# Mixture of experts in one block: sort inverted by one-hot products, rows gathered and scattered tile by tile

## The chip, the cores and the metric

One core of a Trainium2 chip runs the whole kernel. It has TensorE (PE; its weight loads are shown as PEld), VectorE (DVE), ScalarE (ACT), GpSimd (POOL) and SyncE (SP), each with an instruction queue of its own, and 16 DMA engines that all of them can start transfers on. The metric is the device time of one execution in microseconds (us), lower is better.

## The reference

The kernel runs eight stages over 4096 tokens (16 sequences of 256) of 128 channels. Two of the eight, the second and the fourth, are the same mixture of experts; they share their weights. Names and sizes are those of the inputs.

```
feats  = layernorm(x)                                  # (4096, 128)
scores = feats @ centroids.T                           # (4096, 8)
expert = argmax(scores, axis=1)
alpha  = sigmoid(sum(feats * centroids[expert]))
h      = layernorm(feats) * gamma[expert] + beta[expert]
y      = feats + relu(h @ W1[expert].T + b1[expert]) @ W2[expert].T + b2[expert]
x      = x + alpha * y + (1 - alpha) * feats
```

W1 and W2 are 512x128 and 128x512 for each of the 8 experts, all float32. With feats taken out of y, the last line is x + feats + alpha * (relu(...) @ W2.T + b2), which is how the kernel forms it.

## The kernel before

The tokens lie in SBUF as `env.X`, 32 blocks of 128 tokens (NT = 32), and in chunks of four blocks (NC_ = 8). Each stage ends with `sweep` (line 31), a barrier of all engines. Within the expert stage (tags e1 and e3, `experts`, line 865) there are blocks that end with a barrier each:

- `row_scales` (135): DVE and ACT work out mean, scale and shift of each token from its statistics. SP issues five small parameter loads, and behind them the 16 loads of W1 and W2; the block waits for the small ones.
- `turn_weights` (97): two transposes of small parameters.
- `choose` (914): DVE normalises rows chunk by chunk, TensorE transposes them (line 271), ACT copies them out of PSUM, TensorE forms the scores (938), and DVE finds the best expert (967 to 979).
- `place` (982): TensorE counts the tokens per expert and block (1011) and then transposes all weights (1018), ACT copies those out of PSUM (1031). DVE works out each token's slot in an order sorted by expert, every expert's run padded to whole tiles of 128 (1061 to 1079), 40 tiles in all (NJ = 40). It waits before that for memsets of POOL (1035 to 1040). Then it normalises the rows again (1081), and POOL scatters them to the DRAM buffer `sorted_rows` with 32 indirect transfers (1047). In the first stage the buffer is cleared before (1103). SP reads the sorted rows back as `ZS` (1109). Meanwhile beta is folded into b1 by 32 products (1023) and gamma into W1 by DVE (1092, 1093).
- `sorted_experts` (1113): the 40 tiles, in a loop of two tiles per round. TensorE in order: `turn(j + 1)` transposes the next tile's rows (1135), `first(j)` makes the 512 hidden values (1145), `second(j - 1)` the output (1157) and adds b2 by one more product with a row of ones (1159). ACT copies the tile's rows (1189), evacuates the transpose (1202), does half of the relu (1181) and copies b2 and W2 of the tile's expert (1195, 1196). DVE copies b1 and W1 of the expert (1229, 1230), does the other half of the relu (1179) and copies the finished tile to `YS` (1234). SP stores `YS` in four parts to `sorted_out` (1261).
- `collect` (1265): POOL gathers the tokens' rows out of `sorted_out` with 32 indirect transfers (1278), four per chunk; DVE waits for each chunk and adds it, scaled, to X (303, 314), and forms the next statistics (320).

Waits are by semaphores: `need` puts the wait on the following instruction, `hold` on an instruction of its own. `Link` makes each DVE step wait for the one before it. Each engine runs its queue in order, so an instruction that waits holds up all behind it.

## Time and profile before

| | us |
|---|---|
| median of 3 runs | 3189.96 (3188.9 to 3190.61) |
| the profiled execution | 3196.09 |
| its span in the trace | 3194.4 |
| first expert stage (e1) | 661.0 to 926.0 |
| second expert stage (e3) | 1330.2 to 1588.8 |
| TensorE busy | 2303.7 (72%) |
| DVE busy | 2372.1 (74%) |
| ACT busy | 1595.5 (50%) |
| POOL busy | 1677.2 (53%) |

How to read the rows: a row of the timeline has start, busy time, engine, line, operation, what it writes `<-` what it reads, partitions x elements, and how many instructions were merged (float products on TensorE count twice, since they take two passes). In brackets stands the idle time of the engine before it and what ended it. Times are us from the span's start. "Issue" in a bracket is time in which the engine waited for nothing that the profile shows. In the stretches, each engine's busy time and number of instructions is given, then the granted TensorE clock as a share of 2.4 GHz (0.50 is 1.2 GHz).

### The profile page before, as it was taken

How to read it: one execution, taken by the hardware profiler on the slowest of the kernel's cores; microseconds unless marked ns; L12 is line 12 of the kernel's file. 1: busy time of each engine (PE TensorE's matmuls, PEld its weight loads, DVE VectorE, ACT ScalarE, POOL GpSimd, SP SyncE). 2: the span in 40 equal slices, each digit the busy share in tenths (PEclk: the TensorE clock that was granted, in tenths of full speed). 3: DMA queues.
4: the chain of work that ended last, by engine and by line, in shares of the span. 5: the costliest groups of instructions: out<-in, count | busy, mean ns of one | idle time of the engine just before them, and what ended most of it. 6: DMA issues, size and time to landing. Idle time of an engine off the chain costs nothing. (4 is left out here: it accounts for less than half of the span.)

```text
span 3194.4 us, 60389 instructions
## 1 busy us (share of the span) xinstructions
PE 2303.7 (72%) x16660; PEld 1733.3 (54%) x16660; DVE 2372.1 (74%) x5812; ACT 1595.5 (50%) x3215; POOL 1677.2 (53%) x1416
## 2 busy tenths in 40 slices
PE   6727777764929999749244887588888656888887
PEld 2302222343818888638243665476777534777676
DVE  4469999843556666535458886599999876999998
ACT  2356666522715555327223555366666533666665
POOL 0079999703030000040325555499999503999996
PEclk9959999966959999859677999699999956999999
DMA  1000000022110000120100000100000000000000
GB/s 47 0 0 1 0 0 0 1 86 59 32 54 1 0 0 0 54 59 22 51 1 1 1 0 1 30 1 0 0 0 0 3 0 1 1 0 0 0 0 27
DMA packets 61386, 42.73 MB, mean 13 GB/s; under 512 B 7795, under 2 KB 55940, under 8 KB 61190
## 3 DMA queue, kind: packets, MB, share of 16 engines
q1 hardware_dynamic: 56070, 32.09, 3.5%
q0 software_dynamic: 4096, 8.40, 0.9%
q10 hardware_dynamic: 1120, 1.06, 0.1%
q8 instruction: 44, 0.72, 0.1%
q14 instruction: 56, 0.46, 0.0%
HBM read 27.38 MB, written 14.16 MB: 13 GB/s over the span
## 5 line engine op out<-in xcount | busy, mean ns | idle before, releaser
L1631 POOL TENSOR_TENSOR k7a_psums<-k7a_sims 128x1024 f32<-128x1024 f32 x224 | 423.2, 1915 | 189.4 <-ACT k7a_sims L1737 159.2
L1631 POOL TENSOR_TENSOR k5a_psums<-k5a_sims 128x1024 f32<-128x1024 f32 x224 | 423.1, 1915 | 78.2 <-ACT k5a_sims L1737 47.5
L1691 PE MATMUL k7a_pw<-g_ident,k7a_w 128*128 128x128 f32 x2048 | 272.6, 279 | 87.9 <-DVE k7a_hid L1823 47.9
L1691 PE MATMUL k5a_pw<-g_ident,k5a_w 128*128 128x128 f32 x2048 | 273.1, 279 | 86.8 <-DVE k5a_hid L1823 47.9
L755 POOL TENSOR_TENSOR mc_hc<-mc_h,mc_cs 128x512 f32<-128x512 f32 x256 | 319.9, 1270 | 12.7 <-PE mc_y L645 5.1
L728 DVE TENSOR_TENSOR_SCAN mc_h<-mc_dA,mc_dbu 128x512 f32<-128x512 f32 x256 | 304.6, 1208 | 0.0
L1691 PEld LDWEIGHTS k5a_pw<-g_ident,k5a_w 128*128 128x128 f32 x2048 | 224.1, 142 | 147.2 <-DVE k5a_w L1814 91.5
L1691 PEld LDWEIGHTS k7a_pw<-g_ident,k7a_w 128*128 128x128 f32 x2048 | 223.4, 141 | 148.1 <-DVE k7a_w L1814 92.3
L1814 DVE SCALAR_TENSOR_TENSOR k5a_w<-k5a_psums,k5a_best,k5a_lift 128x1024 f32<-128x1024 f32 x224 | 279.4, 1271 | 0.6 <-ACT k5a_lift L1752 0.2
L1814 DVE SCALAR_TENSOR_TENSOR k7a_w<-k7a_psums,k7a_best,k7a_lift 128x1024 f32<-128x1024 f32 x224 | 279.2, 1271 | 0.2
L1752 ACT ACTIVATE k7a_lift<-k7a_psums 128x1024 f32<-128x1024 f32 x224 | 227.8, 1027 | 87.2 <-DVE k7a_w L1814 85.9
L1752 ACT ACTIVATE k5a_lift<-k5a_psums 128x1024 f32<-128x1024 f32 x224 | 227.8, 1027 | 86.0 <-DVE k5a_w L1814 84.7
L645 PE MATMUL mc_y<-mc_hc,g_ident 128*128 128x512 f32 x512 | 242.9, 597 | 11.8 <-DVE m_sz L710 11.6
L1035 POOL MEMSET e3l_keep<- 128x256 f32 x1 | 0.3, 313 | 450.9 <-POOLq L918 450.9
L675 ACT ACTIVATE mc_dA<-m_delta,m_A 128x510 f32 (+1 forms) x256 | 176.7, 690 | 118.6 <-DVE mc_h L728 118.3
L1278 POOL DMA_INDIRECT e_YS<-sorted_out,e_slot x64 | 60.6, 947 | 258.8 <-PEq L1268 239.9
L2155 ACT ACTIVATE r4a_pr<-r4a_pst 128x384 f32<-128x384 f32 x256 | 111.6, 488 | 121.0 <-PE r4a_pst L2311 119.7
L2221 POOL TENSOR_SCALAR_AFFINE_SELECT r4a_pr<-r4a_pr 128x256 f32<-128x256 f32 x256 | 103.0, 420 | 120.4 <-ACT r4a_pr L2155 120.3
L632 PE MATMUL mc_B<-m_bc,g_sel 96*128 (+1 forms) x128 | 50.4, 393 | 157.3 <-ACT mc_cs L687 87.8
L632 PEld LDWEIGHTS mc_B<-m_bc,g_sel 96*128 96x128 bf16 x128 | 12.4, 97 | 253.3 <-issue 122.5
L645 PEld LDWEIGHTS mc_y<-mc_hc,g_ident 128*128 128x128 f32 x512 | 96.6, 190 | 97.5 <-issue 59.1
L2428 DVE TENSOR_REDUCE r4a_nm<-r4a_work 128x2 f32<-128x512 f32 (+1 forms) x192 | 121.4, 682 | 19.7 <-PE r4a_work L2282 19.5
(591 smaller groups left out, 6160.3 us busy)
## 6 DMA issues: line engine op xcount, KB each, us to landing
e_ZS<-sorted_rows SPq DMA_DIRECT2D x8, 640.0 KB, 7.1
sorted_out<-e_YS SPq DMA_DIRECT2D x8, 640.0 KB, 3.6
e1p_w<-in_L_ffn_W_dram SPq DMA_DIRECT2D x16, 256.0 KB, 5.2
e3p_w<-in_L_ffn_W_dram SPq DMA_DIRECT2D x16, 256.0 KB, 5.4
sorted_rows<-e_ZS SPq DMA_DIRECT2D x1, 2560.0 KB, 10.8
g_X<-in_L_attn_a_x_dram SPq DMA_DIRECT2D x8, 256.0 KB, 6.3
out_dram<-g_X SPq DMA_DIRECT2D x1, 2048.0 KB, 8.7
sorted_rows<-e_YS,e_slot POOLq DMA_INDIRECT x64, 2.2
```

The source lines that it names most:

```text
L632: nc.tensor.matmul(Bp[:, s % 2, :], env.sel[:, s, :], bc[:, cols], start=True, stop=True)
L645: nc.tensor.matmul(yp[:, h, :], env.ident[:, :], hc[:, q % RH, :], start=(s == 0), stop=False,).then_inc(summed, 1)
L675: nc.scalar.activation(dA[:, q % RD, :, 1:SEQ], d[:, :, 1:SEQ], ACT.Exp, scale=A[:, h, s:s + 1]).then_inc(decay, 1)
L728: nc.vector.tensor_tensor_scan(h_[:, q % RB, :], dA[:, q % RD, :, :].rearrange("p s t -> p (s t)"), dbu[:, q % RI, :], 0.0, ALU.mult, ALU. ...
L755: nc.gpsimd.tensor_tensor(hc[:, q % RH, :], h_[:, q % RB, :], cs[:, s % 2, :], ALU.mult).then_inc(outs, 1)
L1631: nc.gpsimd.tensor_tensor(psums[:, h - 1, :, :], rows_of(p, h), s2, ALU.add).then_inc(pooled, 1)
L1691: ins = nc.tensor.matmul(pw[:, j, :], w[:, h % WR, j * P:(j + 1) * P], env.ident[:, :], start=(h == 0 and j % 4 == 0), stop=(h == HD - 1 a ...
L1752: nc.scalar.activation(lift[:, h % LR, :], sums_of(h), ACT.Relu).then_inc(lifted, 1)
L1814: nc.vector.scalar_tensor_tensor(w[:, h % WR, :], sums_of(h), best[:, p, h, 7:8], lift[:, h % LR, :], ALU.is_ge, ALU.mult).then_inc(weighe ...
L2155: nc.scalar.activation(pr[:, h, :, :].rearrange("p b c -> p (b c)"), pst[:, h % 2, 0:3 * P], ACT.Exp).then_inc(expd, 1)
L2221: nc.gpsimd.affine_select(pr[:, h, 0:3:2, :], pr[:, h, 0:3:2, :], [[0, 2], [1, P]], ALU.is_ge, 0.0, base=0, channel_multiplier=-1).then_in ...
L2428: nc.vector.tensor_reduce(dst, src, AX, ALU.max, negate=True).then_inc(maxed, 1)
```

## The change

- **One block.** `choose`, `place`, `sorted_experts` and `collect` become one block per stage, with no barrier inside; loops over chunks and blocks are written out. POOL's short memsets come at once, the clearing of the DRAM buffer is gone.
- **Weights kept.** `expert_weights` loads and transposes the weights in the first stage only, and keeps them in SBUF until the last expert stage. Of the 16 groups of four transposes, four are issued ahead of the counts (EARLY), the rest behind them. b2 is loaded to all partitions.
- **The sort is inverted on TensorE.** Instead of scattering rows to slots, the kernel works out which token stands in each slot: a slot is split into tile and place; `hotq` says for each block which tile a token goes to, times its token number plus one (POOL multiplies), `hotr` which place. 32 products of 128x128 by 128x40, summed in PSUM, give `ids`, and from it `token`: row 0 for reading (empty slots read row 0), row 1 for writing (empty slots go to rows that nobody reads).
- **Gather and scatter beside the products.** The normalised rows `zn` go to DRAM by token. Per tile, POOL gathers its rows by token number to one of four buffers `zs` (RZ = 4), and scatters the finished tile to `token_out`. POOL's order is gather 0 to 3, then scatter(j), gather(j + 4) for each j.
- **In the tile loop**, now four tiles per round, gamma and beta are applied by the ACT step that evacuates the transpose (per-partition scale and bias in `affine`, which DVE copies for each tile), ACT no longer copies the rows, and b2 is added by DVE when it evacuates the output, not by TensorE. ACT's `hold` before it copies b2 and W2 is on `kept`, no longer on `summed`.
- **Return.** DVE applies keep and shift to all of X in place; when the last scatter has landed, SP loads the outputs, in token order, in eight transfers, and DVE adds them.

```diff
+    if env.expert_weights is not None:
+        row_scales(nc, env, tag + "sc", second)
+        return env.expert_weights, None
...
-            for t in range(NT):
-                pool.wait_ge(formed, t + 1)
-                nc.gpsimd.indirect_dma_start(env.sorted_rows[:, :], bass.IndirectOffsetOnAxis(slot[:, t:t + 1], 0),
-                                             rows[:, t, :], None).then_inc(scattered, 16)
...
+            pool.wait_ge(vec, SPLIT)
+            nc.gpsimd.tensor_tensor(hotq[:, :, :], hotq[:, :, :], over(env.steps[:, 2, 0:NT], NJ),
+                                    ALU.mult).then_inc(spread, 1)
+
+            def gather(j):
+                need(pool, zturned, j + 1 - RZ)
+                nc.gpsimd.indirect_dma_start(zs[:, j % RZ, :], None, env.token_rows[:, :],
+                                             bass.IndirectOffsetOnAxis(token[:, 0, j:j + 1], 0)
+                                             ).then_inc(gathered[j % RZ], 16)
+
+            def scatter(j):
+                pool.wait_ge(kept, j + 1)
+                nc.gpsimd.indirect_dma_start(env.token_out[:, :], bass.IndirectOffsetOnAxis(token[:, 1, j:j + 1], 0),
+                                             ys[:, j % RZ, :], None).then_inc(stored[j % RZ], 16)
+
+            pool.wait_ge(rowed, 16 * NC_)
+            pool.wait_ge(vec, TOKEN)
+            for j in range(RZ):
+                gather(j)
+            for j in range(NJ):
+                scatter(j)
+                if j + RZ < NJ:
+                    gather(j + RZ)
...
+            pe.wait_ge(spread, 1)
             for t in range(NT):
+                pe.wait_ge(compared, t + 1)
+                nc.tensor.matmul(ids[:, 0:NJ], hotr[:, t % (NT // 2), :], hotq[:, t, :], start=(t == 0),
+                                 stop=(t == NT - 1)).then_inc(found, 1)
...
-                nc.tensor.matmul(po[:, p, 0:P], ones[:, :], b2s[:, p, :], start=False, stop=True).then_inc(summed, 1)
...
+                nc.scalar.activation(zT[:, p, :], pz[:, p, 0:P], ACT.Identity, bias=affine[:, p, 1:2],
+                                     scale=affine[:, p, 0:1]).then_inc(z_in, 1)
...
+            def keep_rows(it, z):
+                j = it * RZ + z
+
+                need(dve, stored[z], 16 * it)
+                need(dve, summed, j + 1)
+                nc.vector.tensor_tensor(ys[:, z, :], po[:, z % 2, 0:P], b2s[:, z % 2, :], ALU.add).then_inc(kept, 1)
...
+            for z in range(RZ):
+                sp.wait_ge(stored[z], 16 * (NJ // RZ))
+            for n in range(NC_):
+                ts = slice(n * TPC, (n + 1) * TPC)
+                sp.dma_start(own[:, ts, :], outs[:, ts, :]).then_inc(loaded[n], 16)
```

On POOL, what stands in a row in the first expert stage before, from the last memsets to the end of the stage (`e_slot` are the slots, `e_YS` the rows):

```order
-L1037 MEMSET e_ones 1x128
-L1038 MEMSET e_ZS 128x5120
-L1040 MEMSET e1l_keep 128x8
-L1047 DMA sorted_rows<-e_YS,e_slot 5120x128 x32
-L989 UNCONDITIONAL_BRANCH
-L1275 UNCONDITIONAL_BRANCH
-L1278 DMA e_YS<-sorted_out,e_slot 128x128 x32
```

and now, up to the third tile:

```order
+L1111 MEMSET e_keep 128x8
+L1114 TENSOR_TENSOR e_hotq<-e_hotq,g_steps 128x1280
+L1119 DMA e_zs<-token_rows,e_token 128x128 x4
+L1125 DMA token_out<-e_ys,e_token 9216x128
+L1119 DMA e_zs<-token_rows,e_token 128x128
+L1125 DMA token_out<-e_ys,e_token 9216x128
+L1119 DMA e_zs<-token_rows,e_token 128x128
```

The large memset has gone, all scatters used to stand before the tiles and all gathers behind them, and now they alternate through the tiles.

On TensorE, from the counts of the first expert stage to the first tile, before:

```order
-L1011 MATMUL e1l_counts<-e1p_hot,g_ranks 128x256 x2
-L1018 MATMUL e1l_turned<-g_ident,e1p_w 128x128 x64
-L1023 MATMUL e1l_shifts<-e_byexpert,e_w1T 128x8 x32
-L989 UNCONDITIONAL_BRANCH
-L1129 UNCONDITIONAL_BRANCH
-L1135 MATMUL e1e_pz<-g_ident,e1e_zs 128x128 x2
-L1145 MATMUL e1e_ph<-e1e_zT,e1e_w1s 128x128 x4
```

and now, up to the output of the first tile (`e_hotr`, `e_hotq` are the one-hots, `e_po` their sum):

```order
+L973 MATMUL e_ph<-g_ident,e_w 128x128 x16
+L991 MATMUL e_ph<-e_hot,g_ranks 128x256 x2
+L973 MATMUL e_ph<-g_ident,e_w 128x128 x48
+L999 MATMUL e_po<-e_hotq,e_hotr 128x40 x32
+L1010 MATMUL e_pz<-g_ident,e_zs 128x128 x2
+L1021 MATMUL e_ph<-e_zT,e_w1s 128x128 x4
+L1010 MATMUL e_pz<-g_ident,e_zs 128x128
+L1021 MATMUL e_ph<-e_zT,e_w1s 128x128 x4
+L1034 MATMUL e_po<-e_w2s,e_hid 128x128 x4
```

16 of the weight transposes have moved ahead of the counts, the 32 products with 8 columns are replaced by 32 with 40, and within a tile the order turn, first, second is as before, without the product for b2.

## Rows read from the trace of the kernel before

**Rows 1.** The head of the page: span and number of instructions.

```profile
span 3194.4 us, 60389 instructions
```

**Rows 2.** Stretches of e1: bounds, length, busy us (instructions) of PE, PEld, DVE, ACT, POOL, clock, DMA.

```profile
698.40:773.00 74.60, 23.95 (x132) 21.55 (x131) 24.16 (x70) 12.54 (x67) 36.66 (x37) 0.57 0.34 99
773.00:875.50 102.50, 101.43 (x760) 91.31 (x760) 54.56 (x200) 75.63 (x239) 0.00 (x0) 0.97 0.06 20
875.50:926.00 50.50, 0.00 (x0) 0.00 (x0) 25.07 (x96) 0.00 (x0) 30.30 (x32) 0.52 0.20 55
```

**Rows 3.** The same stretches of e3, and the end of its scale steps (timeline).

```profile
1330.20:1344.50 14.30, 0.39 (x2) 0.28 (x2) 3.31 (x18) 1.92 (x4) 0.00 (x0) 0.56 0.80 247
1367.30:1437.00 69.70, 23.86 (x131) 21.44 (x131) 24.61 (x70) 12.58 (x67) 36.46 (x37) 0.57 0.24 68
1538.40:1588.80 50.40, 0.00 (x0) 0.00 (x0) 25.11 (x96) 0.00 (x0) 30.32 (x32) 0.52 0.20 55
...
1334.21 0.19 DVE L187 SCALAR_TENSOR_TENSOR g_rnorm<-e3sc_tmp,g_rstd 128x32 f32<-128x32 f32 x1
```

**Rows 4.** Timeline of e1, one steady tile: start, busy, engine, line, operation.

```profile
819.29 0.33 PE L1135 MATMUL e1e_pz<-g_ident,e1e_zs 128*128 128x128 f32 x1
819.46 1.06 PE L1145 MATMUL e1e_ph<-e1e_zT,e1e_w1s 128*128 128x128 f32 x8
820.35 1.06 PE L1157 MATMUL e1e_po<-e1e_w2s,e1e_hid 128*128 128x128 f32 x8
821.34 0.48 PE L1159 MATMUL e1e_po<-e1e_b2s,e_ones 1*128 1x128 f32 x2
821.75 0.33 PE L1135 MATMUL e1e_pz<-g_ident,e1e_zs 128*128 128x128 f32 x1
...
822.02 0.29 DVE L1234 COPY e_YS<-e1e_po 128x128 f32 x1
```

**Rows 5.** Timeline of e1, DVE from the choice of the expert to the slots.

```profile
700.73 0.42 DVE L977 TENSOR_TENSOR e1p_hot<-e1r_sc,e1r_m 128x256 bf16<-128x256 f32 x1
...
707.14 0.42 DVE L1061 COPY e1l_per<-e1l_counts 128x256 f32<-128x256 f32 x1 [5.76 <-POOL e1l_keep L1040]
...
712.21 0.18 DVE L1079 CAST e_slot<-e1l_slotf 128x32 int32<-128x32 f32 x1
```

**Rows 6.** Groups by form, POOL: count | busy us, mean ns | idle before.

```profile
L575 POOL TENSOR_TENSOR m_du<-m_delta,m_u 128x1024 f32<-128x1024 f32 x4 | 10.3, 2579 | 9.5 <-DVE m_delta L594 9.5
```

**Rows 7.** Timeline of TensorE, products with few columns in two stages.

```profile
2016.73 7.01 PE L1305 MATMUL k5w_out<-k5p_keysT,k5p_wq 128*128 128x32 f32 x32 [0.77 <-PEq L101]
...
714.93 11.45 PE L1023 MATMUL e1l_shifts<-e_byexpert,e_w1T 128*128 128x8 f32 x64 [0.35 <-ACT e_w2T L1031]
```

**Rows 8.** Timeline of e1, return: fourth gather of a chunk, and DVE's steps.

```profile
884.05 0.95 POOL L1278 DMA_INDIRECT e_YS<-sorted_out,e_slot  x1 [0.30 <-issue]
...
886.59 1.12 DVE L303 TENSOR_SCALAR e1c_kept<-g_X,g_keep,g_shift 128x128 f32<-128x128 f32 x4 [11.09 <-DMA e_YS<-sorted_out,e_slot]
887.74 1.18 DVE L314 SCALAR_TENSOR_TENSOR g_X<-e_YS,e_alpha,e1c_kept 128x128 f32<-128x128 f32 x4
...
888.95 0.87 DVE L320 BATCH_NORM_STATS2 g_stats<-g_X 128x6 f32<-128x128 f32 x4
```

**Rows 9.** DMA issues: count, size of each, median us from issue to landing.

```profile
e1p_w<-in_L_ffn_W_dram SPq DMA_DIRECT2D x16, 256.0 KB, 5.2
```

**Rows 10.** Timeline of e3: first normalised rows, and the first scatter.

```profile
1381.57 0.35 DVE L1081 TENSOR_SCALAR e_YS<-g_X,g_mean,g_rnorm  x1 [0.37 <-DVE e_slot L1079]
...
1382.72 1.01 POOL L1047 DMA_INDIRECT sorted_rows<-e_YS,e_slot  x1 [6.86 <-DVE e_YS L1081]
```

**Rows 11.** Timeline of e1: a scatter beside DVE steps in SBUF, and one without.

```profile
728.95 0.96 POOL L1047 DMA_INDIRECT sorted_rows<-e_YS,e_slot  x1 [0.31 <-DVE e_YS L1081]
...
730.12 0.47 DVE L1093 TENSOR_SCALAR e_w1T<-e_w1T,e_byexpert 128x512 f32<-128x512 f32 x1
730.21 1.21 POOL L1047 DMA_INDIRECT sorted_rows<-e_YS,e_slot  x1 [0.30 <-issue]
```

**Rows 12.** Stretches in other stages: PE's busy time and the granted clock.

```profile
948.00:960.00 12.00, 9.45 (x34) 6.32 (x34) 7.15 (x26) 5.90 (x10) 0.00 (x0) 0.50 0.00 0
2045.00:2048.00 3.00, 0.87 (x8) 0.80 (x8) 2.31 (x4) 2.95 (x4) 3.00 (x3) 1.00 0.00 0
```

More of the change, by code:

```diff
@@ new lines, in experts, with after, before, over @@
+        loaded = [sem(f"loaded{n}") for n in range(NC_)]
+        back = Back(nc, env, sb, ps, sem)
+        block = outer.enter_context(nc.Block())
+        HOT, ARG, COUNTS, SPLIT, TOKEN = 6, 7, 16, 23, 30
+        EARLY = 4
+        own = zn
+        def after(it, z):
+            return (it, z + 1) if z + 1 < RZ else (it + 1, 0)
+        def before(it, z):
+            return (it, z - 1) if z else (it - 1, RZ - 1)
+        def over(x, n):
+            return x.rearrange("p (k o) -> p k o", o=1).broadcast_to([P, x.shape[1], n])
@@ L982, in place @@
-def place(nc, env, tag, hot, slot, expert, ZS, rows, ones, NJ, weights):
-    NT = env.NT
-    E, J, BANKS = 8, 4, 4
-    fetched, landed, turns, w1T, b1, gT, bT = weights
-    with ExitStack() as ctx:
-        sb, ps, sem = scope(nc, ctx, tag + "l")
-        per, incl, at = sb("per", [P, E, NT]), sb("incl", [P, E, NT]), sb("at", [P, E, NT])
-        keep = sb("keep", [P, E, NT])
-        above = sb("above", [P, E, NT])
-        tiles, ends, one8, first = sb("tiles", [P, E]), sb("ends", [P, E]), sb("one8", [P, E]), sb("first", [P, E])
-        below = sb("below", [P, NJ, E - 1])
-        slotf, expertf = sb("slotf", [P, NT]), sb("expertf", [P, NJ])
-        counts, turned, shifts = ps("counts", [P, 2, 512]), ps("turned", [P, BANKS, 512]), ps("shifts", [P, E, J, E])
-        counted, set_, vec, formed, scattered, loaded, cleared, placed, evacuated, shifted, folded = (sem(x) for x in (
-            "counted", "set", "vec", "formed", "scattered", "loaded", "cleared", "placed", "evacuated", "shifted",
-            "folded"))
-        block = ctx.enter_context(nc.Block())
-        CLEAR = not env.sorted_rows_written
-        env.sorted_rows_written = True
-        GROUPS = 4
-        @block.tensor
-        def _(pe):
@@ L1256, in _ @@
[L1256 to L1287 removed]
+            rows = env.token_rows.rearrange("(t p) c -> p t c", p=P)
@@ L1290, in products @@
+            for n in range(NC_):
+                sp.wait_ge(loaded[n], 16)
 def products(nc, env, tag, items):
```

495 lines of the change are left out of this document (236 added, 259 removed).

## The prediction

> **What bounds the kernel now.** The kernel is a chain of stages with a barrier of all engines between them, so an expert stage is worth exactly what its own chain takes of the 3194.4 us [rows 1]. I read the busy time by stretches first, to cut the two expert stages (e1 from 661.0 to 926.0, e3 from 1330.2 to 1588.8) into routing, tiles and return. In e1 the scores end at 698.4, and the first tile's transpose starts at 773.0: 74.6 us, in which no engine but POOL is busy for half the time [rows 2]; in e3 the same is 69.7 us, and 14.3 us pass before its first normalised rows [rows 3]. The 40 tiles take 102.5 and 101.4 us with TensorE busy throughout. The return takes 50.5 and 50.4 us (875.5 to 926.0; in e3 from 1538.4 to the stage's end at 1588.8), and POOL issues 32 gathers in it [rows 2].
>
> Then I read the order of time inside the three. A steady tile takes TensorE 2.46 us: transpose (0.17 from its start to the next), first product 0.89, second 0.99, bias product and what follows 0.41 [rows 4]. So the tile loop is TensorE's; everything else in the stage is waiting for a chain over DVE, POOL and DMA.
>
> **Routing (front).** The change deletes the scatter of 32 row blocks, the reading back of the sorted rows, the shifts and scaling of W1, and the clearing. What is left in e1 from the end of the scores: choosing the expert ends 2.75 us after 698.4; the counts then stand behind 16 weight transposes that TensorE takes first, so that DVE's next step starts at about +4.5 (before it was 707.14, held by a memset on POOL) [rows 5]. From there to the slots it is 712.39 - 707.14 = 5.25 [rows 5]. New: four small linked steps at about 0.22 (a cast is 0.18 [rows 5], and its wait), and a comparison of 1280 elements, which at DVE's pace in [rows 5] (256 in 0.42, some 1 element per ns) is 1.5: 2.4 together. POOL's product of 1280 elements: 1024 take 2.58 [rows 6], so 3.1 (from 2.4 to 3.6). Then 32 float products with 40 columns, two passes each. The nearest rows are 32 passes of 32 columns in 7.01, 0.219 each, and 64 passes of 8 columns in 11.45 straight behind the weight transposes, 0.179 each [rows 7]. I take 11.4 for e1, which comes out of its transposes in the same way, and 14.0 for e3, which has none before. The 32 comparisons on DVE (at most 0.28 each by the 128x128 steps of [rows 8]) hide behind them. Token numbers: four small steps and a wait, 1.2. First gather: 0.80 until POOL starts it, 2.54 until it has landed (both below). Sum for e1: 4.5 + 5.25 + 2.4 + 3.1 + 11.4 + 1.2 + 3.3 = 31.2 against 74.6: **-43.4**. For e3 33.5 (2.6 more for the products, no transposes ahead of the counts) against 69.7: -36.2. Because the weights are kept, e3 also loses the wait for parameter loads and SP's 16 weight issues: the scale steps alone end at 1334.4 [rows 3], 4.2 after 1330.2, and with about 0.9 for the barrier that is 5.1 instead of 14.3: -9.2. In e1 the loads stay (b2 is moved behind the small ones), nothing is gained. Front of both: **-88.8**. The scores themselves stay TensorE's with the same passes; unrolled and in one block they may gain or lose 1.
>
> **Return (tail).** Before, POOL issued 32 gathers, one per 1.25 us, and DVE waited for each group of four. Now the rows are already in token order, and SP loads them with eight plain transfers. After the last kept tile DVE has 32 steps on X: four in 1.12 [rows 8], so 8.9, then eight chunks of 1.18 + 0.87 + gaps = 2.1 [rows 8], 16.8, and 1.2 to the next stage. Sum 26.9 against 50.5 and 50.4: **-47.1**. What covers the transfers: the last scatter starts 0.8 later and lands within 2.5, a 256 KB transfer lands in 5.2 [rows 9], so the first chunk is there after 8.5, just before DVE is through with X; if that cover fails it costs 1 to 3 per stage.
>
> **Tiles.** Here the change takes off and adds. Off: the bias product (0.41 on TensorE; its addition moves into DVE's evacuation, which takes the place of a copy of 0.29 [rows 4]) and ScalarE's copy of the rows. Scale and bias ride on the ScalarE step that was a copy. If TensorE alone decided, a tile would take 2.05. Added: 40 gathers and 40 scatters on POOL, strictly in the order scatter(j), gather(j+4). Their issue alone is 0.95 + 0.30 and 1.01 + 0.30 [rows 8, 10], or 2.56 per tile, already above 2.46. But there is a longer wait. scatter(j) waits for kept(j); gather(j+4) is queued behind it on POOL, although its data and buffer are long ready. TensorE's turn(j+4) waits for that gather, and behind turn(j+4) on TensorE are queued first(j+3) and second(j+2). DVE waits for second(j+2) to keep tile j+2, and that releases scatter(j+2). So one round of this chain spans **two** tiles:
> - TensorE from turn to the end of second: 0.17 + 0.89 + 1.06 = 2.12 [rows 4];
> - to DVE's start 0.20 (821.82 to 822.02), and its evacuation 0.29 [rows 4];
> - DVE's end to POOL's start of a scatter: 0.80 (1381.92 to 1382.72) [rows 10];
> - the scatter's issue, until the gather can start: 1.31, and 1.51 while DVE copies in SBUF, as it does there with the next W1 (POOL 1.21 instead of 0.96 busy beside such steps) [rows 10, 11]; I take 1.40;
> - the gather from its start to the engine that waits for it: 884.05 to 886.59, 2.54 [rows 8].
>
> Sum 7.35, or 3.68 per tile, and 147 us for 40 tiles (the first four are prefetched, but the pipeline fills at the low clock; I set one against the other). Against 102.5 and 101.4: **+90.1**. Bounds: if of the 0.80 only the usual 0.30 of a queued issue remains and the scatter is 1.31, 6.8, or 3.4 per tile; if both DMAs are slowed by DVE and register waits on TensorE add 0.3, 8.0, or 4.0 per tile. That is -22 and +26 on the total.
>
> What the skill adds here: the Trainium skill, "SBUF — State Buffer", section "SBUF: two separate sides", says that DVE's fast copies and POOL share one pair of ports as an exclusive lock for the whole instruction, and that descriptors written by POOL starve meanwhile. The trace agrees in kind (1.21 for 0.96); by the rule a whole such step (0.47 [rows 11]) could be added per round instead of 0.09, which would make the total 15 us longer. The Trainium skill, "DMA: Bandwidth & Descriptors", section "Anatomy of one DMA — SWDGE (gpsimd) path", gives about 2.0 us plus bytes over 436 GB/s per transfer, an estimate of 2.15 us for 64 KB; the row shows 2.54, and by the page the total would be 16 us shorter.
>
> **The sum.** The profiled execution is 3196.09 us (span 3194.4); the median is 3189.96, 6 lower, and I subtract from the median. -88.8 - 47.1 + 90.1 = -45.8, so 3190 - 46 = **3144**. The larger constant table loaded at launch and the longer unrolled code get at most 1 to 3.
>
> **Rivals.**
> - POOL's issue is the bound, not the round: the latencies overlap in some way I don't see. Then a tile takes 2.56, the loops take 102 each as before, and the total is 3190 - 136 = 3054. For it: four row buffers look like enough. Against: the queue order on POOL, which puts each gather behind a scatter that waits. Chance 6%; another 5% for something between 2.6 and 3.4 (3115 to 3060).
> - Slower: TensorE's clock. Its granted clock is 0.97 in the tiles of before [rows 2], where TensorE never pauses. Now it pauses 1.5 us in every 3.7. If it falls to 1.2 GHz, 2.12 becomes 4.24, the round 9.5, a tile 4.74 and a loop 190: 85 us more, **3229**. Everything above breaks even at 4.25 per tile. For it: a stretch of 12 us with TensorE 79% busy stayed at 0.50 [rows 12]. Against: a stretch of 3 us with only 0.87 busy kept 1.00 [rows 12], so pauses of this length don't take the clock away once it is there, and the first tiles come from prefetched rows with no pause, in which it should rise. Chance 13%.
> - The routing is not as short as I make it: POOL's product and DVE's comparisons disturb each other, the 40-column products run like full ones. At most 8 us per stage, 3160; inside my range.
>
> **Chances.** The forecast's own case (3.4 to 4.0 per tile, front and tail within 8) 71%, giving 3112 to 3179. Between 4.0 and 4.25 per tile 5%. The range has to take in part of the slow case's side: 3105 to 3200. About 0.2% is what a measurement of this kernel tells from no change. Faster by more 0.83, within 0.03, slower 0.14.
>
> **What would show it.** In the profile after: the first gather of e1 some 28 us after the scores; the same tile lines spaced 3.7 us with TensorE idle until the DMA of the gathered rows; POOL idle until DVE's kept tile, twice per round; 26 to 28 us from the last kept tile to the next stage. Wrong if the tiles are 2.5 apart with POOL never idle (first rival), or if TensorE's granted clock in them reads below 0.7 (second).

## The result, and the profile after

The changed kernel takes 3150.7 us (median of four runs, 3144.65 to 3151.4) beside 3189.57 us before: ratio 0.987, 95% interval 0.9856 to 0.9883. That is 38.9 us less; 45.8 were forecast (3144 us), and the range of 3105 to 3200 holds it. The profiled execution has a span of 3149.2 us, 45.2 less than the one before [rows 1]; the one before lay 6.5 us above its median (3196.09), so the profile shows more gain than the medians do.

The stretches of the profile answer to [rows 2, 3] (bounds, length, busy us and instructions of PE, PEld, DVE, ACT and POOL, granted clock, share of the DMA engines, GB/s): first front, tiles and return of the first expert stage, then of the second.

```profile
662.00:730.50 68.50, 45.26 (x228) 42.02 (x228) 33.02 (x118) 17.26 (x30) 5.34 (x6) 0.57 0.35 101
730.50:883.00 152.50, 104.51 (x680) 94.13 (x680) 61.61 (x235) 73.23 (x200) 76.85 (x77) 0.88 0.13 33
883.00:909.00 26.00, 0.00 (x0) 0.00 (x0) 24.27 (x97) 0.00 (x0) 0.97 (x1) 0.56 0.30 86
1314.30:1371.90 57.60, 34.58 (x163) 33.54 (x163) 32.76 (x117) 7.86 (x13) 5.17 (x6) 0.52 0.14 38
1371.90:1521.40 149.50, 101.64 (x680) 90.61 (x680) 62.20 (x235) 72.64 (x200) 76.94 (x77) 0.91 0.13 34
1521.40:1547.30 25.90, 0.00 (x0) 0.00 (x0) 24.15 (x96) 0.03 (x1) 1.03 (x1) 0.56 0.31 86
```

Set against the bounds of before (front 661.0 to 773.0 and 1330.2 to 1437.0, tiles 102.5 and 101.4, return 50.5 and 50.4):

| part | forecast | measured, both stages |
|---|---|---|
| front | -88.8 | -43.5 and -49.2: -92.7 |
| tiles | +90.1 | +50.0 and +48.1: +98.1 |
| return | -47.1 | -24.5 and -24.5: -49.0 |
| sum | -45.8 | -43.6 |

The other 1.6 us of the 45.2 lie outside the two stages. The tiles take back some two thirds of what the front and the return give, so most of the study looks at them.

What the tile loop waits for stands in the answers on two of its lines: the transposes of gathered rows (TensorE's matmul records alone, and what ended its waits ahead of them: us, times), and the scatters (count | busy us, mean ns | POOL's idle time ahead of them, and what ended it):

```profile
L1010 PE MATMUL e_pz<-g_ident,e_zs x80: 272/328/477, 730.6 to 1514.5; 128*128 128x128 f32 x80
its engine sat idle before it (us, times) until:
  DMA e_zs<-token_rows,e_token: 101.2, 62
```

```profile
L1125 POOL DMA_INDIRECT token_out<-e_ys,e_token x80 | 79.2, 990 | 126.1 <-DVE e_ys L1227 123.0 <-issue 3.0
```

TensorE waits for the gathered rows (101.2 of the 302 us of the two loops), POOL waits for the evacuated ones (123.0): neither is busy throughout, which is the mark of a ring, and not of an engine that is full. One turn of it at the full clock (timeline of the first stage: start, busy, engine, line, operation; tile j's evacuation, its scatter, the gather queued behind it, the transpose that this gather releases):

```profile
748.67 0.33 PE L1010 MATMUL e_pz<-g_ident,e_zs 128*128 128x128 f32 x1 [1.45 <-DMA e_zs<-token_rows,e_token]
749.97 1.06 PE L1034 MATMUL e_po<-e_w2s,e_hid 128*128 128x128 f32 x8
751.13 0.29 DVE L1227 TENSOR_TENSOR e_ys<-e_po,e_b2s 128x128 f32<-128x128 f32 x1 [0.35 <-PE e_po L1034]
751.70 0.99 POOL L1125 DMA_INDIRECT token_out<-e_ys,e_token  x1 [1.43 <-DVE e_ys L1227]
753.00 0.97 POOL L1119 DMA_INDIRECT e_zs<-token_rows,e_token  x1 [0.30 <-issue]
755.96 0.33 PE L1010 MATMUL e_pz<-g_ident,e_zs 128*128 128x128 f32 x1 [1.80 <-DMA e_zs<-token_rows,e_token]
```

748.67 to 755.96 is 7.29 us for two tiles. Over whole loops the scatters are 3.74 and 3.66 us apart on average.

### The profile page after: what moved, and what is told of

The parts are those of the page before. It is cut to its first block and busy times, and to the rows that moved or that the text cites. A ratio compares the mean times of both kernels' runs of the same rounds, so it can differ in the third digit from the quotient of the medians.

```text
span 3149.2 us, 59016 instructions
## 1 busy us (share of the span) xinstructions
PE 2296.4 (73%) x16434; PEld 1728.9 (55%) x16434; DVE 2378.4 (76%) x5875; ACT 1574.1 (50%) x3022; POOL 1709.6 (54%) x1446
## 3 DMA queue, kind: packets, MB, share of 16 engines
q10 hardware_dynamic: 1120, 1.22, 0.2%
## 5 line engine op out<-in xcount | busy, mean ns | idle before, releaser
L1125 POOL DMA_INDIRECT token_out<-e_ys,e_token x80 | 79.2, 990 | 126.1 <-DVE e_ys L1227 123.0
```

The source lines that it names most:

```text
L1125: nc.gpsimd.indirect_dma_start(env.token_out[:, :], bass.IndirectOffsetOnAxis(token[:, 1, j:j + 1], 0), ys[:, j % RZ, :], None).then_inc(s ...
```

## Experiments

The kernels ran in three groups of four, each group on one chip, and the three chips are different ones, here called A, B and C. The kernel before took 3204.8, 3193.8 and 3192.7 us on them. That turned out to matter, so totals are compared inside a group where that is possible, and it is said where not. Each version was traced once on its chip. Two of them leave something out of the result, to find a cause: the plain copy leaves out b2, the fixed expert the choice of the expert for VectorE's copies. "Loop" below is from the first transpose of gathered rows to the end of the last evacuation.

| kernel | chip | loops, us | clock in them | median, us | ratio to before (95%) |
|---|---|---|---|---|---|
| gather first | A | 128.6, 128.4 | 0.93, 0.94 | 3104.07 | 0.969 (0.9674 to 0.9706) |
| eight buffers | A | 127.8, 127.3 | 0.93, 0.94 | 3099.76 | 0.9674 (0.9657 to 0.969) |
| filled pauses | A | 144.2, 145.3 | 0.98, 0.97 | 3136.1 | 0.9789 (0.9773 to 0.9805) |
| weights loaded again | A | 150.3, 149.2 | 0.91, 0.91 | 3156.41 | 0.9854 (0.9836 to 0.9872) |
| X steps early | B | 153.4, 148.7 | 0.88, 0.92 | 3144.07 | 0.9839 (0.9823 to 0.9855) |
| eight buffers, copies early | B | 100.0, 99.6 | 0.97, 0.97 | 3041.17 | 0.9522 (0.9506 to 0.9538) |
| eight buffers, plain copy | B | 104.8, 105.5 | 0.97, 0.97 | 3055.92 | 0.957 (0.9554 to 0.9586) |
| eight buffers, fixed expert | B | 98.7, 98.9 | 0.98, 0.97 | 3042.09 | 0.9526 (0.951 to 0.9542) |
| changed kernel again | C | 145.9, 149.1 | 0.93, 0.91 | 3145.0 | 0.9858 (0.9841 to 0.9874) |
| eight buffers again | C | 105.5, 105.6 | 0.97, 0.97 | 3053.32 | 0.9565 (0.9549 to 0.9581) |
| eight buffers, copies early, again | C | 98.9, 99.2 | 0.97, 0.97 | 3045.25 | 0.9541 (0.9525 to 0.9557) |
| all together | C | 97.9, 97.0 | 0.96, 0.96 | 3039.08 | 0.9516 (0.95 to 0.9532) |

### Is it the ring? Gather first, and eight buffers

```diff
             for j in range(NJ):
-                scatter(j)
                 if j + RZ < NJ:
                     gather(j + RZ)
+                scatter(j)
```

> Edit: on GpSimd's queue gather(j+4) now stands ahead of scatter(j) instead of behind it; nothing else. Theory ROUND (the tile loop is set by the ring scatter(j), gather(j+4), turn(j+4), second(j+2), evacuation, scatter(j+2), which spans two tiles): with the gather behind scatter(j-1) instead, the ring of some 7.0 us spans three tiles, 2.35 each, which is below GpSimd's own 1.25 + 1.3 per tile, so GpSimd becomes the bound. Scatter-to-scatter falls from the 3.74 and 3.66 us measured to 2.6, the two loops from 152 and 150 us to about 106 each, total 3060 us (3050 to 3075), TensorE's granted clock in the loops 0.95 or more. Rival THROUGHPUT (the DMA issues and landings themselves are slow in the loop, or the clock is what holds it): the pace stays above 3.4 us per tile and the total within 20 us of 3151.

```diff
-    E, F, RZ = 8, 512, 4
+    E, F, RZ = 8, 512, 8
```

> Edit: eight row buffers instead of four for the gathered and the evacuated rows (RZ = 8), order of GpSimd's queue unchanged. Theory ROUND: gather(j+8) behind scatter(j) makes the ring span six tiles, so it can't bind; the pace falls to GpSimd's 2.6 us per tile and the total to about 3060 us (3050 to 3075), the same as with the other order. If the two edits differ, something beside the ring counts: buffers as such, or the pause that the order leaves. Rival THROUGHPUT: above 3.4 us per tile, total within 20 us of 3151.

Both took some 22 us off each loop, beside the same loop on the same chip (weights loaded again). The totals are 47 and 51 us below 3150.7, which is of another chip; 90 were expected. The ring was there, for neither edit makes any instruction cheaper, and the first changes the order of POOL's queue alone. But the pace did not reach POOL's. In both, the scatters came alternately about 2.56 and 3.80 us apart (with the gather first some of the long ones 4.4). The timeline of eight buffers shows the long one. Columns as above; POOL first, then TensorE and VectorE ahead of the late scatter.

```profile
775.51 0.99 POOL L1125 DMA_INDIRECT token_out<-e_ys,e_token  x1 [1.53 <-DVE e_ys L1227]
776.80 0.97 POOL L1119 DMA_INDIRECT e_zs<-token_rows,e_token  x1 [0.30 <-issue]
778.07 0.99 POOL L1125 DMA_INDIRECT token_out<-e_ys,e_token  x1 [0.30 <-issue]
779.36 0.97 POOL L1119 DMA_INDIRECT e_zs<-token_rows,e_token  x1 [0.30 <-issue]
781.90 0.99 POOL L1125 DMA_INDIRECT token_out<-e_ys,e_token  x1 [1.57 <-DVE e_ys L1227]
```

```profile
778.78 1.13 PE L1034 MATMUL e_po<-e_w2s,e_hid 128*128 128x128 f32 x8 [0.33 <-ACT e_w2s L1081]
779.74 0.27 PE L1010 MATMUL e_pz<-g_ident,e_zs 128*128 128x128 f32 x1
779.85 1.07 PE L1021 MATMUL e_ph<-e_zT,e_w1s 128*128 128x128 f32 x8
780.76 1.13 PE L1034 MATMUL e_po<-e_w2s,e_hid 128*128 128x128 f32 x8
781.33 0.29 DVE L1227 TENSOR_TENSOR e_ys<-e_po,e_b2s 128x128 f32<-128x128 f32 x1 [2.11 <-PE e_po L1034]
```

The evacuation at 781.33 can't be that of the second product that starts at 780.76, since this one is not over: it belongs to the one that starts at 778.78, which TensorE had left for its transpose at 779.74. VectorE had done nothing for 2.11 us, and started 2.55 after that product's start and 1.97 after the gather of 779.36. Two explanations were left: VectorE's evacuation is held by something that goes with POOL's issue of a gather, or a second ring over two tiles binds (evacuation, register load of the expert's number, weight copies, ScalarE's step, both products).

### A second ring, or VectorE held by POOL? Three edits to eight buffers

```diff
                     j = it * RZ + z
-                    if not (last and z == RZ - 1):
-                        stage(*after(it, z))
                     need(dve, made, 2 * j + 2)
...
                     relu(dve, z % 2, 1).then_inc(relu_d, 1)
+                    if not (last and z >= RZ - 2):
+                        stage(*after(*after(it, z)))
...
             stage(0, 0)
+            stage(0, 1)
```

> Edit to the version with eight row buffers (which took 127 us per loop, scatters alternately 2.56 and 3.80 us apart, where 2.56 throughout was expected): VectorE copies the next expert's weights one tile earlier, behind tile j's ReLU for tile j+2, so that this copy and the register load of the expert's number ahead of it no longer stand between the evacuation of one tile and the first product of the next but one. Theory STAGE RING (with the DMAs off the ring, another ring over two tiles binds: evacuation of tile j, VectorE's register load 0.6 to 1.2, weight copies 0.7, ScalarE's step 0.46, first product, second product, evacuation of tile j+2, 6.4 us in all): the pace falls to GpSimd's 2.56 us per tile, the loops to some 106 us, the total by 40 to 3060. Rival PORT (GpSimd's issuing itself delays VectorE's evacuation by 1.3 us every second tile, wherever the weight copies stand): the pace stays above 2.9, total above 3085.

```diff
-                nc.vector.tensor_tensor(ys[:, z, :], po[:, z % 2, 0:P], b2s[:, z % 2, :], ALU.add).then_inc(kept, 1)
+                nc.vector.tensor_copy(ys[:, z, :], po[:, z % 2, 0:P]).then_inc(kept, 1)
```

> Edit to the version with eight row buffers: the evacuation of a tile is a plain copy from PSUM, without the addition of the second bias read from SBUF (b2 is left out of the result). Theory PORT (the evacuation comes 2.5 us after the start of the second product instead of 1.16, in every tile that finds a gather of GpSimd under way, because its second operand is read from SBUF beside GpSimd's descriptor writing): the plain copy comes at 1.2, the pace falls to 2.6 to 2.8, total 3060 to 3075. Rival STAGE RING or any cause outside VectorE's operands: nothing changes but 0.01 us per copy, total within 4 us of the version with eight buffers, 3098.

```diff
-                e = dve.value_load(expert[0:1, bass.ds(j, 1)], min_val=0, max_val=E - 1)
+                e = 0
```

> Edit to the version with eight row buffers: VectorE takes expert 0 for its copies of W1, b1, gamma and beta in every tile, so that it loads no expert number from SBUF into a register (the choice of the expert is left out there; all else, ScalarE's own register load too, stays). Theory STAGE RING: the register load's 0.6 to 1.2 us per tile leaves the ring, which falls from 6.4 to about 5.2 per two tiles, GpSimd's 5.12 binds, total 3060 to 3070. Rival PORT: the late evacuation stays, pace above 2.9, total 3085 or more.

All three came to 2.57 us per tile, so each theory had what it had asked for, and together they said nothing. The traces showed why: with the expert fixed, the evacuation is still the addition with b2, yet it starts 1.16 after the start of its second product in the median, however long ago POOL had begun a gather. The delay was not there to be taken away. These three had run on chip B, and eight buffers on chip A.

To find out, the evacuations of all traces were sorted: those for which VectorE had been idle, TensorE ran at the full clock, and the tile became ready (start of the second product plus 1.16, the median lag in most traces; the smallest is 1.09) between 0.45 and 1.45 us after the start of a gather. On chip A 61 of 76 started more than 0.2 us late: mostly at 1.74 to 2.05 us after the gather's start with the gather first and with eight buffers, at 1.48 to 1.64 in the other two kernels. In the first profile of the changed kernel, on chip B and on chip C it is 0 of 85. Loading the weights again leaves the loop's code alone, and is among the late ones (4 of 9), as are the filled pauses (15 of 24); the same order of queues on the other chips gives 0 of 59 (three profiles of the loop as changed). Of eight buffers alone on chip C only one evacuation meets the conditions.

### The same kernels on one chip

> The changed kernel itself once more, on the same chip as the next three. In the first group of experiments VectorE's evacuation came up to 1.4 us after its tile was ready wherever GpSimd was between 0.5 and 1.9 us into issuing a gather (it then started at 1.8 to 1.98 us after the gather's start); in the profile of the changed kernel and in the second group of experiments it started at once at the same offsets. The two groups ran on two different chips. Theory CHIP: the delay belongs to the chip, so here it shows in all four kernels or in none. The total of the changed kernel hardly depends on it, since its evacuations find the gather long issued: 3151 us within 8.

> The version with eight row buffers once more. Theory CHIP: if this chip shows no delayed evacuation, the scatters are no longer alternately 2.56 and 3.80 us apart but 2.57 throughout, loops of some 106 us, total 3055 (3045 to 3065), as the plain copy gave on the second chip, and what the plain copy seemed to bring was the chip. If this chip does show it, 3098 again. Theory CODE (the two-operand evacuation is slow by itself beside eight buffers): 3098 whatever the chip.

> Eight row buffers and the weight copies one tile earlier, once more. If this chip shows no delayed evacuation and the version with eight buffers alone runs at 2.57 us per tile, moving the copies brings nothing in the steady loop and the two differ by under 15 us, from the last tiles alone (there GpSimd issues no gathers: 1.28 us per tile from a backlog instead of 2.19 and 2.85). If it does show it, this version stays at 3041 and the other at 3098: then the moved copies take the evacuation's delay off the ring.

On chip C no evacuation is late, and there the very kernel that took 3099.76 us on chip A takes 3053.32 (3051.84 to 3056.18 beside 3097.0 to 3100.66), with scatters 2.57 apart until the gathers end. Each chip was used in one session, so "chip" stands for the chip or for its state then. From the changed kernel to this is 92 us: what the theory of the ring had asked for (some 90). The plain copy on chip B (3055.92) had brought nothing of its own, as far as two chips can be compared. POOL, with two instructions per tile, is in the steady loop never idle for longer than its own 0.30; the 1.7 below stands among the scatters behind the last gather (818.49) (timeline of eight buffers on chip C, then what POOL waited for ahead of its scatters between 750 and 825):

```profile
768.07 0.99 POOL L1125 DMA_INDIRECT token_out<-e_ys,e_token  x1 [0.30 <-issue]
769.37 0.97 POOL L1119 DMA_INDIRECT e_zs<-token_rows,e_token  x1 [0.30 <-issue]
770.64 0.99 POOL L1125 DMA_INDIRECT token_out<-e_ys,e_token  x1 [0.31 <-issue]
771.93 0.97 POOL L1119 DMA_INDIRECT e_zs<-token_rows,e_token  x1 [0.30 <-PE e_pz L1010]
```

```profile
L1125 POOL DMA_INDIRECT token_out<-e_ys,e_token x30: 963/987/1141, 750.1 to 823.9; - x30
its engine sat idle before it (us, times) until:
  issue: 8.8, 29
  DVE e_ys L1227: 1.7, 1
```

Moving the weight copies is then worth the last tiles alone: 105.5 and 105.6 us of loop become 98.9 and 99.2, because POOL, once it has no more gathers to issue, finds a backlog (scatters 1.28 apart instead of 2.18 and 2.86). 2.18 and 2.86 are also the answer on the second ring: it exists, and takes 5.04 us per two tiles where POOL issues scatters only, just under POOL's 5.14. On chip A the late evacuation lies on it and makes it 6.4 (2.56 and 3.80), which is argued from the timeline: neither the moved copies nor the plain copy ran there, and the gather first by itself ran on no other chip.

The changed kernel itself hardly notices: its evacuations and its gathers alternate in the ring. Its loops take 150.3 and 149.2 us on chip A, 145.9 and 149.1 on chip C, 152.5 and 149.5 in the first profile, and what differs goes with the clock in them (0.91, 0.91; 0.93, 0.91; 0.88, 0.91).

### The clock: filled pauses

```diff
-                need(pe, gathered[z], 16 * it + 16)
                 need(pe, z_in, j - 1)
+                for k in range(3):
+                    nc.tensor.matmul(pz[:, z % 2, 2 * P:3 * P], env.ident[:, :], env.ident[:, :], start=True, stop=True)
+                need(pe, gathered[z], 16 * it + 16)
```

> Edit: three products of the identity with itself (128 columns each, into a part of the transposes' bank that nobody reads) stand ahead of TensorE's wait for each gathered tile, so that TensorE works in what were pauses; extra work, no result uses it. Theory CLOCK (part of the loops' length is time at a granted clock near 0.5): the mean granted clock in the loops rises from 0.88 and 0.91 to 0.97 or more, rounds all take the 7.0 us of the warm ones, 3.5 per tile, and the total falls by some 15 us to 3136. Rival (the clock drops fall into slack of the ring): total within 3 us of 3151. Second rival (the filling lies on the ring): each tile longer by up to 0.7 us, total up to 3180.

In the changed kernel TensorE's clock falls to 1.2 GHz now and again and comes back by itself. Stretches of two microseconds from 752 on (columns as in the first fence: busy, clock third from the end), and the products in them:

```profile
752.00:754.00 2.00, 2.00 (x17) 1.86 (x16) 1.31 (x5) 0.97 (x3) 1.66 (x2) 1.00 0.10 33
754.00:756.00 2.00, 0.20 (x3) 0.05 (x1) 0.82 (x4) 0.82 (x2) 0.99 (x1) 1.00 0.13 37
756.00:758.00 2.00, 1.99 (x9) 1.82 (x10) 0.15 (x1) 0.95 (x3) 0.97 (x1) 0.58 0.21 66
758.00:760.00 2.00, 2.00 (x12) 2.00 (x12) 0.61 (x2) 0.95 (x3) 0.00 (x0) 0.57 0.00 0
760.00:762.00 2.00, 1.85 (x17) 1.66 (x15) 0.67 (x4) 0.00 (x0) 1.07 (x2) 1.00 0.00 0
```

```profile
756.30 2.03 PE L1021 MATMUL e_ph<-e_zT,e_w1s 128*128 128x128 f32 x8
758.12 1.83 PE L1034 MATMUL e_po<-e_w2s,e_hid 128*128 128x128 f32 x8
759.79 0.27 PE L1010 MATMUL e_pz<-g_ident,e_zs 128*128 128x128 f32 x1
759.90 1.06 PE L1021 MATMUL e_ph<-e_zT,e_w1s 128*128 128x128 f32 x8
```

The first product takes 2.03 instead of 1.06 to 1.13. From the transpose to the evacuation it is 4.10 us in this turn (755.96 to 760.06) instead of 2.46 (748.67 to 751.13): the low clock costs it 1.6 us. TensorE had been busy for 0.20 of the two microseconds from 754 to 756, before the fall. With the pauses filled, there is one fall in the second loop. The clock of the first is 1.00 from 750 to its end (873.5), and no scatter in it is over 4.63 us behind the last (7.01 in the changed kernel):

```profile
750.00:860.00 110.00, 90.12 (x699) 80.73 (x698) 48.07 (x184) 54.70 (x152) 60.77 (x61) 1.00 0.13 37
```

The loops are 144.2 and 145.3 us beside 150.3 and 149.2 of the kernel with the same loop on the same chip (weights loaded again): 10 us for both together, where 15 were expected. The medians agree: 3156.41, less the 10.6 us that the loads cost (next section), is 3145.8 beside 3136.1; that 3136 was the expected total is chance, since it was counted from another chip. The clock theory holds, a third smaller; the two rivals fall. The size is loose: four traces of the unfilled loops have 295 to 302 us for both, the shortest with the highest clock in the first loop. The pace at the full clock is 3.5 us per tile (3.51 and 3.54 on average), what the 7.0 of the turns at the full clock give, so the filling adds nothing that shows.

### Keeping the weights: the second stage loads them again

```diff
-                if "experts" not in stages[i + 1:]:
-                    env.expert_stack.close()
+                env.expert_stack.close()
+                env.expert_weights = None
```

> Edit: the second expert stage loads and turns its weights anew, as the first does; undoes the keeping of the weights alone. Theory: the front of the second stage becomes as long as that of the first, 68.5 instead of 56.8 us from the stage's start to the first tile's transpose, so +11.7 us, total 3162 (the forecast had +9.2 for the loads alone). Rival (the loads hide behind the routing and the turning of the weights fills TensorE's waits): +3 or less.

The stretch from the stage's start to the first transpose, against 57.60 with weights kept:

```profile
1310.50:1378.70 68.20, 45.34 (x228) 42.01 (x228) 33.03 (x118) 17.34 (x30) 5.17 (x6) 0.59 0.35 102
```

10.6 us: 10.0 until the first normalised rows (14.7 instead of 4.7) and 0.6 behind them. The turning of the weights hides almost completely behind the routing, in waits of TensorE that are there anyway. The total, 3156.41 where 3162 was expected, can't be set against the changed kernel, which didn't run on chip A. The expectation's 11.7 for this stretch took 56.8 for the 57.6 us of the changed kernel; with it, 10.9 would have been expected. The forecast's 9.2 for the loads was 0.8 short.

### The cover in the return: X steps early

```diff
+            for t in range(NT):
+                nc.vector.tensor_scalar(env.X[:, t, :], env.X[:, t, :], env.keep[:, t:t + 1], env.shift[:, t:t + 1],
+                                        ALU.mult, ALU.add).then_inc(based, 1)
             dve.wait_ge(found, NT)
...
-            for t in range(NT):
-                nc.vector.tensor_scalar(env.X[:, t, :], env.X[:, t, :], env.keep[:, t:t + 1], env.shift[:, t:t + 1],
-                                        ALU.mult, ALU.add).then_inc(based, 1)
             dve.wait_ge(gated, 1)
```

> Edit to the changed kernel: VectorE's 32 steps on X (8.3 us), which stand behind the last kept tile, are moved ahead of its wait for the last of the 32 products that give the token numbers. Theory COVER (the forecast's: in the tail these steps only hide the last scatter and the first load back, 8.5 us): the tail stays within 1 us of its 26.0 and 25.7 us, and the front grows by the part of the 8.3 us that sticks out behind the products, about 2.5 us per stage; total 5 us more, 3156. Rival (the loads are back well before the steps end): each tail shorter by 3 us or more, total 3151 or less.

The rival was nearer. In the changed kernel (timeline, two rows) the first chunk is added right after the X steps; with these out of the way (the next three, of the edited kernel) it is added when it has landed:

```profile
882.98 8.30 DVE L1247 TENSOR_SCALAR g_X<-g_X,g_keep,g_shift 128x128 f32<-128x128 f32 x32
891.21 1.12 DVE L314 SCALAR_TENSOR_TENSOR g_X<-e_zn,e_alpha,g_X 128x128 f32<-128x128 f32 x4
```

```profile
884.25 0.29 DVE L1230 TENSOR_TENSOR e_ys<-e_po,e_b2s 128x128 f32<-128x128 f32 x1 [0.94 <-PE e_po L1034]
887.18 5.08 SPq L1271 DMA_DIRECT2D e_zn<-token_out  x8
889.93 1.14 DVE L314 SCALAR_TENSOR_TENSOR g_X<-e_zn,e_alpha,g_X 128x128 f32<-128x128 f32 x4 [5.39 <-DMA e_zn<-token_out]
```

The chunk is there 2.75 us after its issue and 5.4 after the last evacuation, not 8.5. Each return is 2.7 shorter (23.3 and 23.2 us). The front pays: the token numbers now wait for the X steps, and come 1.3 and 1.6 us later in their stages. Net gain 2.5 us in all, and the spans say 2.5 too (3146.7 and 3149.2, loops equal within 0.1). The medians can't tell so little: the four runs lie 3137.8 to 3148.47.

### All together

Eight buffers, the gather ahead of the scatter, the copies and the X steps early.

> All together: eight row buffers, the gather ahead of the scatter in GpSimd's queue, the weight copies one tile earlier, the steps on X ahead of the token numbers. The tile loop stays at GpSimd's 2.57 us per tile in any case; the order of gather and scatter then gives nothing, the steps on X take 1.2 us per stage as measured: total 2 to 3 us below the version with the weight copies moved, 3038 us. Theory that GpSimd is now the bound: GpSimd waits only 0.3 us between its instructions. Rival (the backlog of evacuated tiles grows): GpSimd idle elsewhere, total above 3045.

3039.08 us, ratio to before 0.9516 (0.95 to 0.9532): as expected, and the fastest of all that ran. It beats both kernels: by 106 us the changed one on the same chip (3145.0). The gather ahead of the scatter seems to give something in these loops: 97.9 and 97.0 beside 98.9 and 99.2, though not in the steady pace. It wasn't tried by itself with eight buffers. Against the version with the copies early (3045.25, 3040.06 to 3046.92; here 3035.01 to 3040.52) the two series just overlap. POOL's waits between 750 and 820, by line:

```profile
L1125 POOL DMA_INDIRECT token_out<-e_ys,e_token x28 | 27.9, 998 | 8.5 <-issue 6.4 <-DVE e_ys L1230 2.1
L1119 POOL DMA_INDIRECT e_zs<-token_rows,e_token x27 | 26.7, 988 | 8.2 <-issue 7.9 <-PE e_pz L1010 0.3
```

55 instructions with 0.30 ahead of each fill the stretch: POOL is the bound.

## The prediction, point by point: right as a whole, with terms that made up for one another

**What bounds.** Right in kind: the ring of scatter, gather, transpose, products and evacuation over two tiles, with TensorE and POOL both idle in it. Eight buffers show it: 92 us less on one chip, where the forecast's price for the queue order was 3144 - 3054 = 90. Eight buffers also change the buffers of the evacuated rows and the tiles per round; the gather first changes the order alone and came to the same on chip A (3104.07 and 3099.76).

**Tiles, +90.1 forecast, +98.1 measured.** The forecast's 3.68 per tile meets the mean of the scatters (3.74 and 3.66), but by luck: its turn of 7.35 was too long for the full clock, and the clock's falls, which its sum left out, make up for that. In the turn shown (7.29) the terms, too, made up for one another:
- TensorE from transpose to the end of the second product: 2.12 forecast, 2.36 measured (748.67 to 751.03). The first product starts 0.33 after the transpose instead of 0.17, and the second 0.97 after the first instead of 0.89. At the full clock it is mostly 0.30 to 0.34 after a transpose that had to wait, and 0.11 after one that followed at once. ScalarE's step (0.46) is no part of it: the first product of this turn uses the rows of the tile before, and ScalarE's step on the new ones comes later (749.47).
- To VectorE's start 0.20 forecast, 0.10 measured; the evacuation 0.29 as forecast.
- VectorE's end to POOL's start: 0.80 forecast, **0.28** measured (751.42 to 751.70), every time that POOL was already waiting. This term was mis-sized most: [rows 10] is the first indirect transfer after a long pause, and the lower bound, 0.30, was right. After the 16 us pause ahead of the first gather it is 0.89 again (726.73 to 727.62).
- The scatter's issue 1.40 forecast, 1.30 measured.
- Gather to landing: 2.54 forecast, 2.6 median (2.5 to 3.7), 2.96 in the turn shown.

With the median gather a turn is 6.93, and the filled pauses show 7.0 at the full clock, 3.5 per tile: inside the bounds of 3.4 to 4.0. Set at 3.5, 39 intervals and the 6.9 us until the first scatter make 143 us per loop; the rest up to 152.5 and 149.5, 9 and 6 us, is put down to the clock. The filled pauses give 6.1 and 3.9 for it on chip A, so some 5 us of the two loops are not shown to be the clock's. The forecast had set the filling of the pipeline against the prefetch and had given the clock a rival of its own, all or nothing.

**The rival with the slower clock** came true in part. Its price was for a loop at 1.2 GHz throughout, but the clock falls for a few microseconds and comes back (756.3 to some 759.8 in the rows above), and the means are 0.88 and 0.91. The row that was to speak against it, a stretch of 3 us with TensorE 0.87 busy that kept 1.00 [rows 12], was true and proved too little: there the clock was kept, while here it fell at 756.3 after 3 us with TensorE 1.19 busy.

**The rival with POOL as the bound** (3054) was refused for the right reason. Once the ring is opened the measured total is just that, 3053.32 on chip C.

**Front, -88.8 forecast, -92.7 measured.** In the first stage 68.6 was forecast and 68.5 measured; the terms again make up for one another. The rows of the second half of the chain:

```profile
702.01 0.42 DVE L1164 COPY e_per<-e_ph 128x256 f32<-128x256 f32 x1 [1.07 <-PE e_ph L991]
...
707.94 1.49 DVE L1187 TENSOR_TENSOR e_hotq<-g_steps,e_block 128x1280 f32<-128x1280 f32 x1
709.51 2.34 POOL L1114 TENSOR_TENSOR e_hotq<-e_hotq,g_steps 128x1280 f32<-128x1280 f32 x1 [32.16 <-DVE e_hotq L1187]
712.08 13.85 PE L999 MATMUL e_po<-e_hotq,e_hotr 128*128 128x40 f32 x64 [2.52 <-DVE e_hotr L1193]
```

The comparison of 1280 elements is 1.49 (1.5 forecast). POOL's product is 2.34, not 3.1: scaled by elements from 1024 in 2.58, it came out under even the lower bound of 2.4. It reads an operand that is broadcast, which the row of the pace did not. The kernel before has a row that is nearer: 1024 elements with one operand broadcast, in 1.915 (count | busy us, mean ns | idle before):

```profile
L1631 POOL TENSOR_TENSOR k7a_psums<-k7a_sims 128x1024 f32<-128x1024 f32 x224 | 423.2, 1915 | 189.4 <-ACT k7a_sims L1737 159.2 <-DVE k7a_w L1814 30.2
```

Scaled by elements it gives 2.39. That the broadcast is the reason fits both rows; no run changed it alone. The 32 products take 13.85 in both stages. Taking 11.4 for the first, "which comes out of its transposes in the same way", was wrong, and the kernel before shows why. The 64 passes of [rows 7] that took 11.45 still had the full clock for 2.7 us; at the low clock 42 of them took 8.78, 0.209 each:

```profile
714.93:717.60 2.67, 2.67 (x24) 2.67 (x24) 1.91 (x6) 0.00 (x0) 0.00 (x0) 0.99 0.75 221
717.60:726.38 8.78, 8.78 (x42) 8.69 (x41) 6.52 (x18) 0.00 (x0) 6.03 (x6) 0.50 0.11 37
```

Now the clock is 0.50 throughout the products in both stages, and 64 passes at 0.216 fit the 0.219 of the 32 columns in [rows 7]. In the second stage 57.6 instead of 61.4: scores in 21.3 (22.8 before), scores to first transpose 31.6 instead of 33.5, first rows at 4.7 instead of 5.1. The loads' price holds nearly: 10.0 by experiment, 9.2 forecast.

**Return, -47.1 forecast, -49.0 measured.** 26.0 and 25.9 instead of 26.9: the X steps take 8.30, not 8.9. The cover was said to hold by a hair (8.5 against 8.9); it holds by 2.7. The load was priced at 5.2 by [rows 9], the median of sixteen weight transfers, and the first of the eight is there 2.75 after its issue; the last scatter starts 0.3 after its evacuation, not 0.8.

## To carry to other kernels

Two transfers in one queue, one that waits for a result and behind it one that feeds the engine that makes the results, can close a ring: write down which instruction each waits for and count the tiles that one turn spans, since the pace is the turn divided by that number, and more buffers or another order raise the number without making anything faster. Before a profile of one chip is read against that of another, run one kernel twice: here the same code differed by 46 us between two chips, and three experiments on the second seemed to confirm two theories about the first. A wait measured at the end of a long pause (0.80) is no price for the same wait in a steady loop (0.28).

## What the hardware showed that was not expected

- **A chip on which VectorE's evacuation comes late behind the start of a gather.** The evacuation adds one operand in PSUM and one in SBUF; on chip A it mostly started 1.5 to 2.05 us after the gather's start when it was ready earlier (61 of 76 cases), on the others it started at once (0 late of 85). VectorE's ReLU steps, which read one operand in PSUM and a bias per partition, met a gather in the same way 76 times on chip A (ready taken as the start of the first product plus 1.17) and started more than 0.2 us late in 6 of them, elsewhere in 0 of 137. So the delay goes mostly with the evacuation. The Trainium skill, "SBUF — State Buffer", section "SBUF: two separate sides", names VectorE's steps with two SBUF inputs, against a GpSimd operation that reads SBUF, among those where the one that starts first keeps the shared ports for the whole instruction. This step has only one SBUF input, and on chip A it waits beyond the 0.97 us of the gather's record; on chips B and C it does not wait. So the rule as stated agrees with chips B and C and does not explain chip A, and the cause stays open. Whether the kernel before pays for it too (3204.8 us on chip A, 3193.8 and 3192.7 on the others) was not traced.
- **Loading the expert's number into a register** leaves VectorE idle for 0.8 us or more ahead of its copies (751.42 to 752.23, from the evacuation's end to the copy of b1; up to 1.25). The load's own record is 0.30 us of that in the median, the rest are steps of the queue before and behind it. The Trainium skill, "DMA: Bandwidth & Descriptors", section "Latency and other measured facts", gives some 600 ns as the floor of a `tensor_load`; here the record is half of it, and the idle time above it. With a fixed expert on chip B the loops are 6.7 us shorter than with eight buffers alone on chip C, as by moving the load and the copies off the ring (6.5 on chip C).
- **TensorE's clock** fell to 1.2 GHz now and again in loops in which TensorE waits a third of the time (101.2 of 302 us, in 62 pauses), and came back within the same loop; keeping it up was worth 10 us of 300.
- **POOL left 0.30 us between two indirect transfers** and took mostly 0.97 to 0.99 for each (up to 1.22 at 761.92, beside VectorE's copy of W1), the same on all three chips: 2.57 us per gather and scatter of 128 rows wherever it had no other wait.
